# Two of three attentions of a decoder block on their own helper: maxima from stacked rows, three score banks, one bank per maximum

## What is computed

```python
# first attention: 16 heads of 16, keys from the context
attn = softmax(einsum('bhqd,bhkd->bhqk', qh, kh) * scale)
x = x + attn @ vh @ Wo + bo
# second (causal, keys are the 2048 tokens) and third (keys are the 1601 context rows)
a = softmax(einsum('bhsd,bhtd->bhst', q, k) * D ** -0.5)
if causal:
    a = a * (arange(t)[None, :] > arange(s)[:, None])   # keys AFTER the query are kept
x_out = x + einsum('bhst,bhtd->bhsd', a, v) @ li1_w + li1_b
```

## Time and profile before

| | us |
|---|---|
| three runs, median | 4732.31 |
| three runs, lowest and highest | 4724.95, 4739.31 |
| the profiled execution, device time | 4742.03 |
| its span, first to last instruction | 4740.3 |
| of it: first attention, score phase (94 to 738) | 644 |
| second attention, prologue and score phase (1281 to 1350 to 2482) | 69 + 1132 |
| third attention, prologue and score phase (2685 to 2752 to 3646) | 67 + 894 |
| PE busy, DVE busy, ACT busy | 3913.5, 2543.0, 2071.0 |

### The profile page before, as it was taken

One profiled execution on the slowest core, in us unless ns is written; L12 is line 12 of the kernel. 1 busy time (PEld: TensorE's weight loads), 2 busy tenths in 40 slices (PEclk: granted clock), 3 DMA queues, 4 the chain that ended last, 5 costly groups with the idle time before them and its releaser, 6 DMA issues. The chain is left out here.

```text
span 4740.3 us, 68737 instructions
## 1 busy us (share of the span) xinstructions
PE 3913.5 (83%) x24838; PEld 1741.1 (37%) x24838; DVE 2543.0 (54%) x3771; ACT 2071.0 (44%) x4092; POOL 966.7 (20%) x530
## 2 busy tenths in 40 slices
PE   5999995299378888888877578888888569999999
PEld 2333333177222222222225312222223346666665
DVE  5777764711455555555525555555552555555554
ACT  1777781011135555555563245555554322222222
POOL 2000001022121110111003056666555300000000
PEclk7999997588687788877868789999999779999999
DMA  1000000267210000000000000000000100000000
GB/s 54 11 12 14 7 5 6 80 215 229 69 26 15 10 17 8 20 9 6 6 5 18 22 22 12 19 10 18 8 8 5 36 29 29 20 27 28 19 19 18
DMA packets 92823, 140.98 MB, mean 30 GB/s; under 512 B 28227, under 2 KB 78346, under 8 KB 85514
## 3 DMA queue, kind: packets, MB, share of 16 engines
q1 hardware_dynamic: 87946, 131.92, 8.8%
q0 software_dynamic: 4608, 5.57, 0.7%
HBM read 98.64 MB, written 9.18 MB: 23 GB/s over the span
## 5 line engine op out<-in xcount | busy, mean ns | idle before, releaser
L589 DVE TENSOR_REDUCE a_part_max<-a_mx 128x2 f32<-128x1024 f32 (+1 forms) x1024 | 1074.5, 1104 | 793.1 <-PE a_mx L693 789.5
L525 ACT ACTIVATE a_e<-a_sc 128x512 f32<-128x512 f32 (+1 forms) x1472 | 806.0, 594 | 573.6 <-PE a_sc L680 571.6
L680 PE MATMUL a_sc<-a_qs,a_ks 97*128 97x512 f16 (+1 forms) x1472 | 514.2, 411 | 93.8 <-ACT a_e L525 36.7
L589 DVE TENSOR_REDUCE xa_part_max<-xa_mx 128x2 f32<-128x802 f32 x512 | 472.1, 986 | 131.3 <-PE xa_mx L693 128.3
L525 ACT ACTIVATE xa_e<-xa_sc 128x512 f32<-128x512 f32 (+1 forms) x832 | 445.5, 596 | 126.3 <-PE xa_sc L680 118.7
L490 POOL TENSOR_TENSOR a_part_sum<-a_part_sum,a_e 128x2048 f32<-128x2048 f32 x96 | 434.4, 4525 | 15.3 <-ACT a_e L525 5.8
L693 PE MATMUL a_mx<-a_khi,a_qhi 32*128 32x512 f16 (+1 forms) x2048 | 292.5, 402 | 153.7 <-DVE a_part_max L589 130.6
L1537 ACT ACTIVATE moe_sg<-moe_gp 128x512 f32<-128x512 f32 (+1 forms) x216 | 128.7, 596 | 608.6 <-PE moe_up L1491 608.6
L1566 DVE TENSOR_TENSOR moe_hf<-moe_sg,moe_up 128x512 f32<-128x512 f32 (+1 forms) x216 | 148.2, 686 | 378.3 <-ACT moe_sg L1537 378.3
L716 PE MATMUL a_po<-a_e,a_v 128*32 128x512 f32 (+1 forms) x2432 | 340.8, 633 | 0.0
L1491 PE MATMUL moe_gp<-moe_xp,moe_wp 128*128 128x512 f16 (+1 forms) x1296 | 316.4, 380 | 28.3 <-DVE moe_wp L1594 28.3
(11 more groups left out here) (301 smaller groups left out, 4499.3 us busy)
## 6 DMA issues: line engine op xcount, KB each, us to landing
experts_w_up<-in_we SPq DMA_DIRECT2D x32, 1024.0 KB, 6.6
...
a_qs<-a_qhi SPq DMA_DIRECT2D x256, 32.0 KB, 1.8
a_ks<-a_khi SPq DMA_DIRECT2D x224, 32.0 KB, 1.9
...
a_qs<-a_low SPq DMA_DIRECT2D x128, 32.0 KB, 1.8
```

The costliest lines, as they stand in the source:

```text
L525: act.activation(e[:r, m % ering, j, :], src[:r, :], ACT.Exp, scale=scale).then_inc(s_taken, 1)
L589: dve.tensor_reduce(part_max[:, 2 * h:2 * h + 2, t, c], src[:, :, :mxw], AX.X, ALU.max).then_inc(m_taken, 1)
L680: pe.matmul(dst[:r, :], ks[rows, g % 2, c, P * kt:P * kt + r], qs[rows, c, n % NQ, :], start=True, stop=True).then_inc(s_ready, 1)
```

## The change

The second and the third attention no longer call `attention` but a new helper, `attention_stacked`:

```diff
-                        attention(nc, a, p, a[p + "_wq"], a[p + "_wk"], a[p + "_wv"], xq, KC, xk, nkk, nkeys, SLOT, n == 0,
+                        attention_stacked(nc, a, p, a[p + "_wq"], a[p + "_wk"], a[p + "_wv"], xq, KC, xk, nkk, nkeys, SLOT ** -0.5, n == 0,
```

```diff
+    tiles = []
+    for n in range(NC):
+        skipped = sum(passed(n, kt) for kt in range(nkt))
+        kept = nkt - skipped
+        tiles += sorted(((n, kt) for kt in range(nkt)),
+                        key=lambda x: (2 * x[1] + 1) * kept if x[1] < skipped else (2 * (x[1] - skipped) + 2) * skipped)
+    place_of = {tile: m for m, tile in enumerate(tiles)}
```

In the new helper the maxima are computed from the stacked rows (96 of them, without the row of the maximum), each by a matmul of its own, into a bank of its own, and reduced by a reduce of its own. `qhi`, `khi`, `raw` and `low` are gone; a buffer `stage` holds both halves. PSUM: three banks `wb` for all work that isn't scores, three banks `sc`, `po` and `pd`. The list `during` holds per chunk the next chunk's work:

```diff
+    nmx = 4
+    mxw = (nkeys + nmx - 1) // nmx
+    mxs = [min(mxw * i, nkeys - mxw) for i in range(nmx)]
+    nvb = (nkt + 3) // 4
+    NC = NG * NCH
+    NST = 3
+    NQ = 3
+    NWB = 3 if ones_at is None else 4
+    NSC = 3
+    PASSED_WORK, TILE_WORK = 5, 8
+    LEAD = 2
+    own_sum = ones_at is None
+    NCOPY = 2 if own_sum else 1
+    den_at = 0 if own_sum else ones_at
+    MOVES = 16 * 3 * HG
...
+    before = [("k", 0, 0), ("q", 0), ("k", 0, 1)]
+    for i in range(nmx):
+        before += maxima(0, [i]) + ([("k", 0, i + 2)] if i + 2 < len(kch) else [])
+        if i == 1:
+            before += [("v", 0, b) for b in range(nvb)] + [("q", 1)]
+    before.append(("turn", 0))
+    during = []
+    for n in range(NC):
+        g, qc = n // NCH, n % NCH
+        work = []
+        if g + 1 < NG:
+            work += {0: [("k", g + 1, c) for c in range(2)], 1: [("k", g + 1, c) for c in range(2, len(kch))],
+                     2: [("v", g + 1, b) for b in range(nvb)]}.get(qc, [])
+        if n + 1 < NC:
+            work += maxima(n + 1) + [("turn", n + 1)]
+        if n + 2 < NC:
+            work.insert(16, ("q", n + 2))
+        if 0 < n < NC - 1:
+            work[26:26], work[32:32] = [("divisors", n - 1)], [("divide", n - 1)]
+        during.append(work)
+    after = [(u, n) for n in (NC - 2, NC - 1) for u in ("divisors", "divide")]
+    order = before + [u for work in during for u in work] + after
+    number = {u: i for i, u in enumerate(order)}
```

```diff
+                    dve.tensor_scalar(high, src[:, :w], bias, None, ALU.add).then_inc(high_ready, 1)
+                    dve.wait_ge(high_ready, m + 1)
+                    last = dve.scalar_tensor_tensor(out=low, in0=src[:, :w], scalar=bias, in1=high, op0=ALU.add, op1=ALU.subtract)
...
+                elif u[0] == "max":
+                    n, t, j, k = u[1:]
+                    dve.wait_ge(unit_ready, i + 1)
+                    dve.tensor_reduce(part_max[:, j, t, k:k + 1], src[:, :mxw], AX.X, ALU.max).then_inc(unit_taken, 1)
...
+            def unit(u):
+                i = number[u]
+                dst = wb[i % NWB]
+                if i >= NWB:
+                    pe.wait_ge(unit_taken, i - NWB + 1)
...
+                elif u[0] == "max":
+                    n, t, j, k = u[1:]
+                    g = n // NCH
+                    if (t, j) == (0, 0):
+                        wait_stacked(pe, ("q", n))
+                        if n % NCH == 0:
+                            for c, (o, w) in enumerate(kch):
+                                if o < mxs[k] + mxw:
+                                    wait_stacked(pe, ("k", g, c))
+                    last = pe.matmul(dst[:, :mxw], qs[:STACK, j, n % NQ, P * t:P * t + P],
+                                     ks[:STACK, g % 2, j, mxs[k]:mxs[k] + mxw], start=True, stop=True)
+                elif u[0] == "divisors":
...
+            def score(n, kt, j):
+                i = HG * (nkt * n + kt) + j
+                r = kt_rows[kt]
+                if i >= NSC:
+                    pe.wait_ge(exp_done, i - NSC + 1)
+                if passed(n, kt):
+                    c, t = kt // TPC, kt % TPC
+                    pe.matmul(sc[i % NSC][:, :], qs[:STACK + 1, j, n % NQ, P * t:P * t + P],
+                              ks[:STACK + 1, n // NCH % 2, j, CH * c:CH * c + CH], start=True, stop=True).then_inc(sc_ready, 1)
+                    return
+                pe.matmul(sc[i % NSC][:r, :], ks[:STACK + 1, n // NCH % 2, j, P * kt:P * kt + r],
+                          qs[:STACK + 1, j, n % NQ, :], start=True, stop=True).then_inc(sc_ready, 1)
```

PE's sequence follows six steps per tile, each with one sixth of the tile's share of the other work:

```diff
+            shares = [1, 1, 1, 1, 1, 1 if own_sum else 0]
+            tile_work = [PASSED_WORK if passed(m // nkt, m % nkt) else TILE_WORK for m in range(nkt * NC + 1)]
+            for m in range(nkt * NC + 1):
+                n, kt = m // nkt, m % nkt
+                ahead = (m + LEAD) // nkt
+                window = range(max(nkt * ahead - LEAD, 0), min(nkt * (ahead + 1) - LEAD, nkt * NC + 1))
+                work = during[ahead] if ahead < NC else []
+                in_all = sum(shares) * sum(tile_work[k] for k in window)
+                def some_work(step):
+                    before_tile = sum(shares) * sum(tile_work[k] for k in range(window.start, m))
+                    lo, hi = (-(-len(work) * (before_tile + tile_work[m] * sum(shares[:i])) // in_all) for i in (step, step + 1))
+                    for u in work[lo:hi]:
+                        unit(u)
+                if kt == 0 and n < NC:
+                    pe.wait_ge(negmax_loaded, 16 * HG * (n + 1))
+                for half in range(2):
+                    if n < NC:
+                        score(n, kt, 2 * half)
+                    some_work(3 * half)
+                    if n < NC:
+                        score(n, kt, 2 * half + 1)
+                    some_work(3 * half + 1)
+                    if m and half == 0:
+                        sum_values((m - 1) // nkt, (m - 1) % nkt)
+                    elif m:
+                        sum_weights((m - 1) // nkt, (m - 1) % nkt)
+                    some_work(3 * half + 2)
+            for u in after:
+                unit(u)
```

328 lines of the change are left out of this document (312 added, 16 removed).

## The result

| | before | after |
|---|---|---|
| median of the runs, us | 4735.81 (4724.95 to 4746.65) | 4533.68 (4527.87 to 4541.17) |
| span of the profiled execution | 4740.3 | 4527.9 |

The ratio is 0.956, with a 95% interval of 0.953 to 0.958: 202 us faster.

What follows compares the result with a forecast made beforehand. It took the first attention as PE bound, the second and third as bound by turns between ACT and PE. Third -94, second -53, prologues +45 make -102: from the median 4732.3 to 4630 us, range 4560 to 4740.

Steps and rivals of the forecast that it cites:

- forecast 49.1 and its share of the projections: Third attention: a chunk takes 49.1 us instead of 55.1, key and value projections add about 25; stage -94 us.
- the rest, 4 x 6.1 = 24: Second attention, four chunks: query projection, divisors, division, turn and small waits at 6.1 us a chunk, taken from the first attention.
- 24 x 2.75 = 66: Second attention, four chunks: 24 passed tiles (keys all before the queries; score and row sum only) at 2.75 us.
- 161: Second attention, four chunks: PE time of 40 kept tiles (keys not all masked) plus 179 maxima at 0.215 us.
- the 53 for key and value projections: Second attention: 53 us added to the stage for key and value projections, from the kernel before.
- 40 x (0.86 + 2.00 + 0.20): Second attention, four chunks: 40 kept tiles, each 0.86 us scores, 2.00 values and weights' sum, 0.20 turns.
- 1079 against 981: Second attention's score phase: forecast 1079 us against 1132 before, a gain of 53.
- For low clock left in kept tiles I add 35: Second attention: 35 us added, a tenth of 643 us at half rate; bounds nil and 150.
- The clock rival: Second attention: half clock stays in passed tiles and kept ones behind them; stage about 1190, total 4741 us; chance 0.13.
- the waits that a third score bank ends: Second and third attention: ACT and PE wait for each other over two score banks; with three, no wait.
- the wide maxima I had as a cost alone: Maxima as single 96-row matmuls instead of packed fours: +136 us PE time in the second attention, about +100 in the third.
- +24 against +45: Prologues of second and third attention: about +25 and +20 us, together +45, bounds +30 to +60.

Runs made afterwards that it cites:

- late_units: Changed kernel with query projection, divisors and division put later in each chunk's work list (places 48, 52, 56 instead of 16, 26, 32); 4565.84 us, 0.963 of before.

## Why the prediction was half right

**Direction, and the third attention.** Right: a chunk of 48.9 to 51.4 us, the first (54.3) and the last two apart (forecast 49.1 and its share of the projections), reduces that follow each other every 0.60 to 0.61 us at 512 columns (0.60 to 0.69), PE idle 29 us in 16 chunks, ACT waiting for POOL 2.9 us in all.

**The first step that failed: "the rest, 4 x 6.1 = 24" beside "24 x 2.75 = 66".** One group of four chunks was priced at 161 + 66 + 24, and the 53 for key and value projections fall in three of the four groups, 17.6 in each: 269 us. The second group took 245:

```profile
1618.70:1690.00 71.30, 69.68 (x448) 20.81 (x446) 48.02 (x78) 35.95 (x67) 5.58 (x5) 1.00 0.09 22
1690.00:1758.10 68.10, 65.58 (x430) 25.19 (x429) 46.94 (x76) 36.93 (x82) 5.08 (x4) 1.00 0.05 13
1758.10:1812.50 54.40, 52.25 (x307) 16.58 (x305) 45.71 (x78) 37.35 (x98) 5.06 (x4) 1.00 0.03 8
1812.50:1863.80 51.30, 47.53 (x234) 15.17 (x232) 42.91 (x73) 38.51 (x115) 4.62 (x4) 1.00 0.04 9
```

The 24 passed tiles took 65.3 us, as forecast, but with other work among them. Of the twelve from 1812.5 to 1844.4, PE's query projection, divisors, division, and the values and the sum of the kept tile before (L1128, L1155, L1160, L1202, L1223; us, PE and PEld busy, clock, DMA):

```profile
1812.50:1844.40 31.90, 1.88 (x4) 0.76 (x4) 1.00 0.05 13
1812.50:1844.40 31.90, 1.05 (x8) 0.97 (x8) 1.00 0.05 13
1812.50:1844.40 31.90, 1.16 (x8) 0.97 (x8) 1.00 0.05 13
1812.50:1844.40 31.90, 1.06 (x8) 0.16 (x8) 1.00 0.05 13
1812.50:1844.40 31.90, 1.07 (x8) 0.16 (x8) 1.00 0.05 13
```

The same stands in the eight, and in the four without divisors and division. From start to start that is 9.0 us of side work and 6.0 of values and sums in a group, which the forecast counts once more, in "the rest" and in the 161: 15 us. I had read that ACT bounds these tiles (2.38) and PE needs 1.55, and did not use the difference as cover. late_units confirms the direction and some 60% of the size for the side work. And that the 66 came out is luck: 2.75 was the middle between ACT's floor and PE at half clock, but the clock was 1.00, and a passed tile without other work took 2.28, 55 us for 24. So the cover wasn't whole: the 15 us of other work lengthened the stretches by some 11, since it stands bunched in a few tiles, and the surplus in 2.75 happened to pay for that.

**The second: "40 x (0.86 + 2.00 + 0.20)".** Four of the ten kept tiles of an average chunk lie on the diagonal, and their values don't run over 512 columns:

```profile
1783.05 0.43 PE L1206 MATMUL a_po<-a_em,a_v 128*32 128x128 f32 x8 [0.16 <-POOL a_em L986]
...
1786.62 0.45 PE L1205 MATMUL a_po<-a_e,a_v 128*32 128x128 f32 x8
1786.84 0.45 PE L1206 MATMUL a_po<-a_em,a_v 128*32 128x128 f32 x8
...
1790.61 0.66 PE L1205 MATMUL a_po<-a_e,a_v 128*32 128x256 f32 x8
1791.06 0.42 PE L1206 MATMUL a_po<-a_em,a_v 128*32 128x128 f32 x8
```

The four cost 2.8 us instead of 4.0, 5 us a group. The projections took 14.4 us from start to start where the price, from busy times, was 17.6. These three make 23 of the 24 us. The three groups with projections were priced at 807 and took 739; the last was priced at 237 and took 241 to the end of the stage. That is 63 of the 98 us that were missed in this stage (1079 against 981).

**The third: "For low clock left in kept tiles I add 35".** The other 35. The clock was 0.97: half clock stood in the first two chunks and the last alone, 43 us in all, which is 21 us lost at most, and these are within the 981 already. So at least 14 of the 35 were too many, and the work was overpriced by 63 to 84. The clock rival had 0.13 and fell: the low clock followed from the old pattern and went with it.

A look at my own numbers would have warned me. The forecast left (1079 - 66 x 4 - 35) / 160 = 4.9 us for a kept tile with its share of side work, where the kernel before took 4.74 (the mean of its 160 kept tiles, from the starts of their exponentials), though I took every wait away. The change made it 4.41.

**The mechanism was only partly the one I told.** I put the gain down to the waits that a third score bank ends, and that bank is worth 15 us in each attention; the wide maxima I had as a cost alone. With the edits made in this order, of the 155 us of the second 70 come from wide maxima and single placing together (31 by the placing alone, 39 by the width on top), 70 from the division of the work, the side work's own banks and the finer order, 15 from the third bank. Of the 84 of the third: 8, 61 and 15. The middle term is one sum of several causes that no run parts, and another order of the edits could give other shares.

**Prologues.** +24 against +45. The wait for the stacked rows is there: the first maxima begin at 1305.35, 12 us later than in the earlier trace rows, 14 from the start of the stage (15 were put), behind

```profile
1305.35 1.98 PE L1148 MATMUL a_wb<-a_ks,a_qs 96*128 96x512 f16 x4 [13.24 <-DMA a_qs<-a_stage]
```

The third's grew by 6 and not by 20: its first score used to wait 10.77 us for the row of maxima and now waits 4.01, which I had not looked at. First attention and the rest: nil, as forecast.
